# Softmax sums inverted in the attention stage, outputs scaled on GpSimd, and the layer norm moved into the group plan of a fused attention and recurrent-FFN kernel

## The chip, the cores and the metric

The kernel runs on one core of a Trainium2 chip. The metric is the device time of one execution in microseconds, the median of the runs shown. The engines are TensorE (PE, with its weight loads as PEld), VectorE (DVE), ScalarE (ACT), GpSimd (POOL) and SyncE (SP), which issues most of the DMAs. The kernel is written out by hand per engine: each engine has its own program, and semaphores order them.

## The reference, cut to what matters

Input x has 4 sequences of 1024 tokens with 1024 features. All of it is float32.

```python
xn = layernorm(x)
# attention: 32 query heads, 8 key/value heads, head size 32, rotary, causal
q, k, v = xn @ wq.T, xn @ wk.T, xn @ wv.T        # q, k rotated
attn = softmax(mask(q @ k.T / sqrt(32)))
s = (attn @ v) @ wo.T
# recurrent FFN on the last token only
thought = layer_norm(xn)[:, -1] @ agg_w + agg_b
for _ in range(4):
    t = gelu(layer_norm(thought) @ d1_w + d1_b)
    thought = thought + t @ d2_w + d2_b
f = layer_norm(xn + sigmoid(xn @ gate_w + gate_b) * (thought @ bc_w + bc_b))
out = x + s * silu(f)
```

## The kernel before, in words

There are three stages, one after the other, each a block with its own buffers.

`project_phase` normalises x, transposes it, and computes q, k and v as sums of three products of rounded parts. It writes the transposed x (`xt_scratch`), q, k and v to DRAM. The change does not touch it.

`attention_phase` runs over 32 groups, a group being one sequence and one key/value head with its 4 query heads (GROUPS, L26). Two groups make a turn of the loop over `c`, four turns (8 groups) make one step `s` of the recurrent FFN, and there are 4 steps. A group has 36 slots. In each slot PE computes one block of scores (`stp`, L985), ACT takes its exponential into `pr` (L796), and whatever `PLAN_TEXT` (L68) lists for the slot follows: `mx` is a product for the row maxima of the next group (PE, L973 to L978) with its maximum on DVE (`row_max`, L861), `pv` the product of probabilities and values into `yp` (L992), `ss` the column sums of the probabilities into the PSUM tile `trp` (L1001), `mt` the transposed maxima, `cy` the copy of `yp` to `ys` on ACT (L765), `fa`/`fb`/`fs`/`ft` the pieces of the FFN's matrix-vector products, and `ge` the gelu on ACT. The maxima have two PSUM buffers (`mxp`): PE may compute maximum k only when DVE has finished k-2 (L969). The scores have two buffers as well. `trp` is one buffer that all of `ss`, `mt`, `fa`, `fb`, `ft` and the layer norm's means share in a fixed order, counted by `tr_full` and `tr_free`; `use` (L564) gives each its number.

POOL adds up the probabilities over the key blocks (`acc`, `acc0`; L721, L739, L749), and `ss` turns the result into sums. ACT copies the sums from `trp` to `sm` (`copy_sums`, L771), and SP stores them to DRAM (`s_scratch`, L607). The outputs `ys` are stored without being divided (`store_y`, L611).

The layer norm of the recurrent state (`th`, 128 x 32 numbers) lies between two steps, outside the plan: after the last group of a step DVE runs `layernorm_sum`, `layernorm_centre` and `layernorm_scale` (L952 to L956), PE multiplies the two sums by a matrix of 1/1024 (`mean`, L1134), and POOL raises the variance to the power -1/2 (`ln_pool`, L712). The result `t_in` is what `fa` needs in slot 3 of the next group.

`output_phase` first loads and splits the two weight matrices in 16 pieces through 4 staging buffers, and then runs over 32 tiles of 128 tokens. For a tile, PE computes `gp` = xn @ gate_w and `op` = y @ wo.T (48 products each, L1385). POOL's queue loads `xa` (the two parts of the transposed x, 1 MB) when `gp` of the tile before is done, and `yr` (the attention output, 0.5 MB) after the second `power` (L1273 to L1279). `xa` has one buffer, `gp` and `op` have two. SP loads x itself (`xs`) and stores the output. The softmax sums are handled here: SP loads 32 rows of sums (`load_sums`), DVE inverts them (`invert`, L1306), SP stores the inverses to `r_scratch` and reads them back spread over 128 partitions (`spread`, L1216, 0.5 MB into `o_rinv`), and DVE multiplies `yr` by them (`normalise`, L1312). Then ACT rounds `yr` into `ya[0]`, and DVE takes the rest into `ya[1]` (L1373), which `op` of the next tile needs. All of DVE's work on a tile stands in one fixed order (L1349 to L1373).

Of the kernel before, what the change touches and what calls it, by code (L numbers as in the profile page):

```python
# [82 lines left out]
14: ss 1  # L83
15: mx 7
16: mx 8
18: mx 9
19: mx 10, ge
20: ss 0, mx 11
# [3 lines left out]
24: pv 1 2  # L92
# [4 lines left out]
31: mx 18, pv 1 4  # L97
33: mx 19
# [23 lines left out]
TRN = 7  # L122
A0 = 6


def build_kernel(nc, x, wqT, wkT, wvT, woT, in_g, in_b, agg_w, agg_b, pn_g, pn_b, d1_w, d1_b, d2_w, d2_b,
# [11 lines left out]
    with ExitStack() as outer:  # L138
        def osb(name, shape, dt):
# [11 lines left out]
        s_d = dram("s_scratch", (REP, 1 + GROUPS, T), F32)  # L151
        r_d = dram("r_scratch", (2, REP * KV, P), F32)
        attention_phase(nc, x, in_g, in_b, agg_w, agg_b, pn_g, pn_b, d1_w, d1_b, d2_w, d2_b, bc_b, pick,
                        q_d, k_d, v_d, y_d, s_d, ident, ident16, mask_q, mask_k, mhalf, bcast)
        output_phase(nc, x, woT, gate_w, gate_b, out_g, out_b, xt_d, y_d, s_d, r_d, ident, mhalf, bcast, out)
# [317 lines left out]
def attention_phase(nc, x, in_g, in_b, agg_w, agg_b, pn_g, pn_b, d1_w, d1_b, d2_w, d2_b, bc_b, pick,  # L473
                    q_d, k_d, v_d, y_d, s_d, ident, ident16, mask_q, mask_k, mhalf, bcast):
# [7 lines left out]
    with ExitStack() as ctx:  # L482
# [18 lines left out]
        sm = [sb(f"sm{i}", [P, HALF], F32) for i in range(2)]  # L501
# [37 lines left out]
        s_out = [sem(f"a_s_out{i}") for i in range(2)]  # L539
# [10 lines left out]
        ln_sum, ln_ve, ln_rs = sem("a_ln_sum"), sem("a_ln_ve"), sem("a_ln_rs")  # L550
# [13 lines left out]
        use = {"fa": 0, ("mt", 1): 1, "fb": 2, "ft": 3, ("ss", 1): 4, ("ss", 0): 5, ("mt", 0): 6}  # L564
# [6 lines left out]
        def _(sp):  # L571
# [35 lines left out]
            def store_sums(half, slot):  # L607
                sp.dma_start(s_d[:, bass.ds(slot, 1), half * HALF:(half + 1) * HALF].rearrange("h a t -> h (a t)"),
                             sm[half][0:P:HD, :]).then_inc(s_out[half], 16)

# [23 lines left out]
            load_w(0, d1_chunk(0))  # L634
            sp.wait_ge(tr_full, 4)
            load_w(1, d1_chunk(0))
# [3 lines left out]
            with sp.Fori(0, STEPS) as s:  # L640
                with sp.Fori(0, CH) as c:
                    for par in range(2):
                        it = s * CH + c
                        n = it * 2 + par
                        nxt = 1 - par
                        tb = trb(s, c, par)
                        sp.wait_ge(st_done, NST * n + 2)
                        load_k(nxt, (n + 1) % GROUPS)
                        load_q(1, nxt, it if par == 0 else (it + 1) % (GROUPS // 2))
                        sp.wait_ge(pv_done, products((1, 7), n))  # L650
                        load_v(nxt, (n + 1) % GROUPS)
                        sp.wait_ge(ys_done, 2 * n + 2)
                        store_y(1, n)
# [813 lines left out]
```

## Time and profile before

| | us |
|---|---|
| median of 3 runs (lowest, highest) | 2888.37 (2877.07, 2893.84) |
| the profiled execution, its own time | 2904.24 |
| the profiled execution's span | 2902.5 |
| PE busy | 2643.2 (91%) |
| DVE busy | 1714.5 (59%) |
| POOL busy | 1297.7 (45%) |
| ACT busy | 1055.4 (36%) |

The projection takes about the first 600 us of the span, the attention stage lasts to about 1990, and the output stage, with its weights first, to the end. The page gives the shares over the whole span; each stage has to be read by itself, with the view that lists the busy time of each engine by stretch. PEclk is the granted clock of TensorE as a share of the full one.

### The profile page before, as it was taken

The numbers are of one execution on the slowest core, as the hardware profiler recorded it, in microseconds if no ns is written. First come the engines' busy times: TensorE is split into PE (matmuls) and PEld (weight loads), VectorE is DVE, ScalarE is ACT, GpSimd is POOL, SyncE is SP. The second block draws the span as 40 slices with busy tenths as digits, with TensorE's granted clock in tenths as the row PEclk, the third lists the DMA queues.
The fourth block names the chain that finished last, engine by engine and source line by source line (L and its number), as shares of the span: only waits on it lengthen the run. The fifth ranks groups of instructions, "written<-read, shape, count | busy, mean of one in ns | idle before, by whom it ended". The sixth has DMA issues, their size and how long they took to land. (4 is left out here: it accounts for less than half of the span.)

```text
span 2902.5 us, 46017 instructions
## 1 busy us (share of the span) xinstructions
PE 2643.2 (91%) x14400; PEld 1712.5 (59%) x14400; DVE 1714.5 (59%) x3448; ACT 1055.4 (36%) x1715; POOL 1297.7 (45%) x562
## 2 busy tenths in 40 slices
PE   5999999969999999999999999995688788898887
PEld 4888888844444444444444444442577676676775
DVE  6455444356555655566556655653666667676666
ACT  2111111106666565665666556662211111111111
POOL 0211211127788678877888688872111111111111
PEclk9999999979999999999999999997799999899998
DMA  6444444365654565556455545564678677567766
GB/s 232 167 175 172 166 173 174 138 201 182 189 154 152 166 189 153 153 167 186 152 156 167 184 152 157 167 189 137 138 123 116 111 123 123 111 124 124 123 114 121
DMA packets 235894, 450.04 MB, mean 155 GB/s; under 512 B 17528, under 2 KB 101720, under 8 KB 235860
## 3 DMA queue, kind: packets, MB, share of 16 engines
q1 hardware_dynamic: 162468, 397.68, 43.3%
q0 software_dynamic: 73392, 51.91, 14.4%
q8 instruction: 21, 0.34, 0.0%
q14 instruction: 13, 0.11, 0.0%
HBM read 334.42 MB, written 114.58 MB: 155 GB/s over the span
## 5 line engine op out<-in xcount | busy, mean ns | idle before, releaser
L867 DVE CUSTOM_DVE_ANT_0 bcast<-mxp,mask_q 128x128 f32<-128x128 f32 (+7 forms) x1054 | 751.9, 754 | 506.4 <-PE mxp L976 283.5
L796 ACT ACTIVATE pr<-stp 128x512 f32<-128x512 f32 x1152 | 670.3, 596 | 529.1 <-PE stp L985 351.6
L985 PE MATMUL stp<-qs,ks 97*128 97x512 f32 x1152 | 522.5, 461 | 19.2 <-ACT pr L796 14.8
L1385 PE MATMUL gp<-g,xa 128*128 128x512 f32 x1536 | 395.3, 421 | 128.9 <-DMA xa<-xt_scratch 117.5
L426 PE MATMUL eo<-xt,w 128*128 128x512 f32 x1920 | 449.2, 393 | 3.6 <-DVE xt L369 3.6
L749 POOL TENSOR_TENSOR acc<-acc,pr 128x2048 f32<-128x2048 f32 x96 | 439.7, 4580 | 24.7 <-ACT pr L796 14.5
L985 PEld LDWEIGHTS stp<-qs,ks 97*128 97x128 f32 x1152 | 214.7, 189 | 384.1 <-ACT pr L796 275.8
L1385 PEld LDWEIGHTS gp<-g,xa 128*128 128x128 f32 x1536 | 313.5, 206 | 210.1 <-issue 108.0
L426 PEld LDWEIGHTS eo<-xt,w 128*128 128x128 f32 x1920 | 359.1, 189 | 77.5 <-issue 4.0
L1385 PE MATMUL op<-o,ya 128*128 128x512 f32 x1536 | 356.2, 391 | 21.6 <-DVE ya L1326 21.6
L1385 PEld LDWEIGHTS op<-o,ya 128*128 128x128 f32 x1536 | 290.3, 189 | 82.6 <-DVE ya L1326 22.0
L997 PE MATMUL yp<-pr,vs 128*32 128x512 f32 (+3 forms) x3088 | 323.1, 498 | 0.0
L1258 POOL DMA_DIRECT2D xa<-xt_scratch x66 | 57.6, 878 | 540.5 <-PE gp L1385 447.2
L975 PE MATMUL mxp<-ks,qs 96*128 96x512 f32 x526 | 244.8, 465 | 3.4 <-DVE mx L867 3.2
L721 POOL TENSOR_TENSOR acc<-acc,pr 128x1536 f32<-128x1536 f32 (+2 forms) x99 | 235.3, 2377 | 16.5 <-PE yp L1077 9.0
L749 POOL TENSOR_TENSOR acc<-pr 128x2048 f32<-128x2048 f32 x32 | 146.7, 4585 | 175.2 <-ACT pr L796 175.2
L291 POOL TENSOR_TENSOR r<-rt,r 128x1024 fp32r<-128x1024 f32 x40 | 95.9, 2398 | 282.1 <-ACT r L322 282.1
L395 DVE TENSOR_TENSOR rt<-eo,cs 128x512 f32<-128x512 f32 x160 | 99.0, 680 | 147.3 <-PE eo L426 147.3
L976 PE MATMUL mxp<-ks,qs 96*128 96x256 f32 (+2 forms) x526 | 172.1, 327 | 0.0
L322 ACT ACTIVATE r<-rt 128x1024 fp32r<-128x1024 f32 x40 | 42.4, 1061 | 356.7 <-DVE rt L399 356.7
L1296 ACT ACTIVATE c<-a 128x1024 f32<-128x1024 f32 x32 | 33.9, 1058 | 343.6 <-DVE a L1363 343.6
L978 PE MATMUL mxp<-ks,qs 96*128 96x256 f32 (+2 forms) x528 | 132.8, 354 | 18.3 <-DMA qs<-q_scratch 16.5
(139 smaller groups left out, 2788.0 us busy)
## 6 DMA issues: line engine op xcount, KB each, us to landing
wch<-in_d_w SPq DMA_DIRECT2D x132, 1024.0 KB, 8.0
qs<-q_scratch SPq DMA_DIRECT2D x201, 256.0 KB, 7.3
xa<-xt_scratch POOLq DMA_DIRECT2D x66, 512.0 KB, 9.0
xt_scratch<-xt SPq DMA_DIRECT2D x16, 2048.0 KB, 14.6
q_scratch<-r SPq DMA_DIRECT2D x64, 512.0 KB, 3.2
o_rinv<-r_scratch SPq DMA_DIRECT2D x33, 512.0 KB
yr<-y_scratch POOLq DMA_DIRECT2D x33, 512.0 KB, 6.5
xs<-in_x SPq DMA_DIRECT2D x33, 512.0 KB, 10.7
```

Of the source, the lines that this page charges most:

```text
L395: last = nc.vector.tensor_tensor(rt[:, o, :], bank[:, e, :], cs[:, s, tok], ALU.mult)
L426: last = nc.tensor.matmul(out, lhs[a](k), rhs[c](k), start=(k == 0 and (a, c) == (0, 0)), stop=(k == KT - 1 and (a, c) == (1, 0)))
L721: nc.gpsimd.tensor_tensor(acc[:, :, c0:HALF], acc[:, :, c0:HALF], pr[1][:, :, at:at + HALF - c0], ALU.add).then_inc(add_done, 1)
L749: nc.gpsimd.tensor_tensor(acc[:], other, pr[1][:, :, at:at + HALF], ALU.add).then_inc(add_done, 1)
L796: nc.scalar.activation(pr[half][:, :, at:at + P], stp[u % 2][:].rearrange("p (h t) -> p h t", h=REP), ACT.Exp, scale=SCALE).then_inc(act_d ...
L867: last = nc.vector.tensor_tensor_reduce(out=bcast[:, k % 2, hh * step:hh * step + w], in0=mxp[k % 2][:, hh * step:hh * step + w], in1=mask ...
L975: nc.tensor.matmul(bank[:, 0:512], lhs, ks[par][0:QR, 0:512], start=True, stop=True)
L976: last = nc.tensor.matmul(bank[:, 512:512 + w], lhs, ks[par][0:QR, 512:512 + w], start=True, stop=True)
L978: last = nc.tensor.matmul(bank[:, hh * step:hh * step + w], lhs, ks[par][0:QR, 0:w], start=True, stop=True)
L985: last = nc.tensor.matmul(bank, ks[par][:, j * P:(j + 1) * P], qs[par][:, :, i * P:(i + 1) * P], start=True, stop=i != j)
L997: last = nc.tensor.matmul(yp[h * HD:(h + 1) * HD, c0:HALF], vs[par][:, j, :], pr[half][:, h, at:at + HALF - c0], start=(j == 0), stop=(j = ...
L1385: last = nc.tensor.matmul(bank[:, cols], lhs[pa][:, k, :], ws[pw][:, k, cols], start=(k == 0 and (pa, pw) == (0, 0)), stop=(k == KT - 1 an ...
```

## The change

- Attention stage. `copy_sums` and `store_sums` are gone, with `sm`, `s_scratch` and `r_scratch`. DVE gets a plan entry `rc` right behind `ss` (slots 14 and 20): a 32x32-block transpose of `trp` (128x512, PSUM) to SBUF, a reciprocal of every 32nd column (16 per partition), and a second 32x32 transpose that reads those 16 numbers broadcast 32 times and writes `rinv` (128x512).
- POOL multiplies `ys` by `rinv` in place (`normalise`), half 1 after its first addition of half 1 and half 0 after the second. SP stores `ys` when that is done, so `store_y` moves behind the second weight burst in SP's order, and one follows `move_mt(0)`.
- The layer norm becomes plan entries of the last group of a step: `ls` in slot 15, `l0` and `lc` in 18, `l1` and `lv` in 24, `lt` in 32. `ln_pool` stands behind POOL's third addition of half 1. For this the loops run over CH-1 turns and the last turn is written out (`turns`).
- SP loads the next keys and queries one score block earlier. The weights of the FFN are still loaded by SP.
- Output stage. `load_sums`, `spread`, `invert` and `normalise` are gone. POOL's order becomes: wait for `y2_done`, load `yr`, wait for `g_done`, load `xa`, the two powers.

The core of the diff (the re-indentation of the loop bodies is left out):

```diff
-14: ss 1
-15: mx 7
+14: ss 1, rc 1
+15: mx 7, ls
-18: mx 9
+18: mx 9, l0, lc
-20: ss 0, mx 11
+20: ss 0, rc 0, mx 11
-24: pv 1 2
+24: pv 1 2, l1, lv
+32: lt
...
+        uses = [{"fa": 0, ("mt", 1): 1, "fb": 2, "ft": 3, ("ss", 1): 4, ("ss", 0): 5, ("mt", 0): 6},
+                {"fa": 0, ("mt", 1): 1, "fb": 2, "ft": 3, ("ss", 1): 4, "l0": 5, ("ss", 0): 6, "l1": 7, ("mt", 0): 8}]
...
@@ SP, one group
+                sp.wait_ge(st_done, NST * n + 1)
...
-                        sp.wait_ge(ys_done, 2 * n + 2)
-                        store_y(1, n)
...
-                        sp.wait_ge(ys_done, 2 * n + 3)
-                        store_y(0, n + 1)
-                        sp.wait_ge(tr_free, tb + use[("ss", 1)] + 2)
-                        store_sums(1, n)
-                        sp.wait_ge(tr_free, tb + use[("ss", 0)] + 2)
-                        store_sums(0, n + 1)
+                sp.wait_ge(yn_done, 2 * n + 3)
+                store_y(1, n)
                 sp.wait_ge(tr_free, tb + use[("mt", 0)] + 2)
                 move_mt(0, nxt)
+                sp.wait_ge(yn_done, 2 * n + 4)
+                store_y(0, n + 1)
@@ POOL
+            def normalise(half, n):
+                pool.wait_ge(ys_done, 2 * n + 3 - half)
+                pool.wait_ge(rc_done, 2 * n + 2 - half)
+                nc.gpsimd.tensor_tensor(ys[half][:], ys[half][:], rinv[half][:], ALU.mult).then_inc(yn_done, 1)
...
                     nc.gpsimd.tensor_tensor(acc[:], other, pr[1][:, :, at:at + HALF], ALU.add).then_inc(add_done, 1)
+                    if j == 1:
+                        normalise(1, n)
+                    if j == 2:
+                        normalise(0, n)
+                    if j == 3 and "l1" in use:
+                        ln_pool(s + 1, tb + use["l1"])
@@ DVE
+            def reciprocals(half, k, tu):
+                dve.wait_ge(tr_full, tu + 1)
+                nc.vector.transpose(sq_t[:].rearrange("p a u -> p (a u)"), trp[:]).then_inc(tr_free, 1)
+                dve.wait_ge(tr_free, tu + 2)
+                nc.vector.reciprocal(rr[half][:], sq_t[:, :, 0]).then_inc(rr_done, 1)
+                dve.wait_ge(yn_done, 2 * k + 2 - half)
+                dve.wait_ge(rr_done, 2 * k + 2 - half)
+                nc.vector.transpose(rinv[half][:], rr[half][:].unsqueeze(2).to_broadcast([P, SPREAD, SQUARE])
+                                    ).then_inc(rc_done, 1)
...
+                        elif e[0] == "rc":
+                            reciprocals(e[1], n, tb + use[("ss", e[1])])
...
+                        elif e[0] == "ls" and "l0" in use:
+                            link(nc.vector.tensor_tensor(th[:], th[:], bc(fvec[:, 3, :], B), ALU.add), base)
+                            layernorm_sum()
+                        elif e[0] == "lc" and "l0" in use:
+                            layernorm_centre(tb + use["l0"], base)
+                        elif e[0] == "lv" and "l1" in use:
+                            layernorm_var(tb + use["l1"])
+                        elif e[0] == "lt" and "l1" in use:
+                            layernorm_scale(s + 1, base)
@@ output stage, POOL
             with pool.Fori(0, TILES) as n:
+                pool.wait_ge(y2_done, n + 1)
+                load_ya((n + 1) % TILES)
                 pool.wait_ge(g_done, n + 1)
                 load_xa((n + 1) % TILES)
                 power(n, 0)
                 power(n, 1)
-                pool.wait_ge(y2_done, n + 1)
-                load_ya((n + 1) % TILES)
@@ output stage, SP and DVE
-                    spread(1 - par, n + 1)
-                    load_sums((n + 2) % TILES)
...
-                    invert(n + 1)
...
-                    normalise(n + 1)
```

## Rows read from the trace of the kernel before

**Rows 1.** Busy time by stretch (us, PE, PEld, DVE, ACT, POOL, clock, DMA share, GB/s).
```profile
760.00:1070.00 310.00, 301.66 (x1909) 141.31 (x1908) 186.43 (x509) 186.66 (x331) 246.60 (x78) 0.98 0.52 160
2052.00:2902.50 850.50, 729.34 (x3024) 591.74 (x3024) 567.67 (x672) 121.01 (x111) 124.44 (x158) 0.92 0.70 118
```

**Rows 2.** Timeline of PE, output stage: start, duration, engine, line, operation, idle before.
```profile
2065.61 11.04 PE L1385 MATMUL gp<-g,xa 128*128 128x512 f32 x48
...
2256.10 12.61 PE L1385 MATMUL gp<-g,xa 128*128 128x512 f32 x48 [6.86 <-DMA xa<-xt_scratch]
2279.90 11.17 PE L1385 MATMUL gp<-g,xa 128*128 128x512 f32 x48 [0.30 <-DMA xa<-xt_scratch]
...
2864.90 11.04 PE L1385 MATMUL gp<-g,xa 128*128 128x512 f32 x48
```

**Rows 3.** The chain of work that ended last, output stage (start, duration, what).
```profile
2003.96 12.91 DMA c<-in_gate_w
...
2240.23 15.74 DMA xa<-xt_scratch
...
2270.58 9.27 DMA xa<-xt_scratch
```

**Rows 4.** Timelines of SP, POOL and DVE, two tiles of the output stage and the end.
```profile
2239.17 0.56 SPq L1221 DMA_DIRECT2D o_rinv<-r_scratch  x1
2241.23 0.41 SPq L1242 DMA_DIRECT2D xs<-in_x  x1
...
2239.37 1.74 POOL L1258 DMA_DIRECT2D xa<-xt_scratch  x2 [12.22 <-PE gp L1385]
2248.27 1.11 POOL L1263 DMA_DIRECT2D yr<-y_scratch  x1 [0.21 <-issue]
...
2257.54 1.22 DVE L1315 TENSOR_TENSOR yr<-yr,o_rinv 128x1024 f32<-128x1024 f32 x1 [6.11 <-DMA yr<-y_scratch]
2291.11 1.23 DVE L1352 TENSOR_TENSOR a<-gp,vecs 128x1024 f32<-128x1024 f32 x1 [0.54 <-PE gp L1385]
2302.90 1.22 DVE L1363 TENSOR_TENSOR a<-a,vecs 128x1024 f32<-128x1024 f32 x1
2894.52 1.22 DVE L1315 TENSOR_TENSOR yr<-yr,o_rinv 128x1024 f32<-128x1024 f32 x1 [5.42 <-DMA yr<-y_scratch]
```

**Rows 5.** Groups by line and shape (count | busy us, mean ns | idle before).
```profile
L874 DVE TENSOR_TENSOR fsb<-trp,fsb 128x512 f32<-128x512 f32 x22 | 15.2, 691 | 10.4 <-PE trp L1029 10.4
L1310 DVE RECIPROCAL o_rcp<-ident 32x128 f32<-32x128 f32 x32 | 29.9, 933 | 0.0
L739 POOL TENSOR_TENSOR acc<-acc,pr 128x512 f32<-128x512 f32 x22 | 28.4, 1289 | 3.5 <-ACT pr L796 3.5
```

**Rows 6.** Timelines of DVE, PE and POOL, slots 15 to 18 of one group.
```profile
1041.12 0.82 DVE L867 CUSTOM_DVE_ANT_0 bcast<-mxp,mask_q 128x640 f32<-128x640 f32 x1 [0.23 <-PE mxp L976]
...
1042.24 0.50 PE L985 MATMUL stp<-qs,ks 97*128 97x512 f32 x1 [0.45 <-ACT pr L796]
1042.58 0.40 PE L975 MATMUL mxp<-ks,qs 96*128 96x512 f32 x1
...
1042.76 4.59 POOL L749 TENSOR_TENSOR acc<-pr 128x2048 f32<-128x2048 f32 x1 [5.48 <-ACT pr L796]
```

**Rows 7.** Timeline of ACT: the copy of slot 13 in three groups, all of parity 1.
```profile
949.34 0.59 ACT L769 ACTIVATE ys<-yp 128x512 f32<-128x512 f32 x1
...
1039.10 0.59 ACT L769 ACTIVATE ys<-yp 128x512 f32<-128x512 f32 x1
...
1119.78 0.59 ACT L769 ACTIVATE ys<-yp 128x512 f32<-128x512 f32 x1
```

**Rows 8.** Timelines of POOL and DVE in the layer norm between two steps.
```profile
974.92 7.28 POOL L721 TENSOR_TENSOR acc<-acc,pr 128x1536 f32<-128x1536 f32 x3
...
974.98 3.44 DVE L856 TENSOR_TENSOR cen<-cen,f_rs 128x32 f32<-128x32 f32 x1 [1.13 <-POOL f_rs L714]
978.46 2.39 DVE L858 TENSOR_TENSOR cen<-cen,fvec 128x32 f32<-128x32 f32 x1
```

More of the change, by code:

```diff
@@ L122 @@
 TRN = 7
+SQUARE = 32
+SPREAD = HALF // SQUARE
 A0 = 6
@@ L751, in _ @@
+            ln_pool(0, 6)
+            pool.wait_ge(init_p, 3)
+            turns(pool, turn)
             late_additions(GROUPS)
+            normalise(1, GROUPS)
         @block.scalar
@@ new lines, in turn @@
+            def turn(s, c, par, use):
+                it = s * CH + c
+                n = it * 2 + par
+                tb = trb(s, c, par)
+                for u, (half, j, i) in enumerate(ST):
+                    act.wait_ge(st_done, NST * n + u + 2)
+                    if u == 0:
+                        act.wait_ge(tr_full, tb)
+                    if u == HALF_ST:
+                        act.wait_ge(pv_done, NPV * n + 1)
+                        act.wait_ge(add_done, NADD * n + 1)
+                    if u == LAST_UNIT[(1, 4)] + 1:
+                        act.wait_ge(tr_full, tb + use[("ss", 1)] + 1)
+                    at, c0 = prob_piece(half, j)
+                    at += i * P - half * HALF - c0
+                    nc.scalar.activation(pr[half][:, :, at:at + P], stp[u % 2][:].rearrange("p (h t) -> p h t", h=REP),
+                                         ACT.Exp, scale=SCALE).then_inc(act_done, 1)
+                    for e in ACT_PLAN[u]:
+                        if e[0] == "fc":
+                            copy_burst(tb + use["fa"])
+                        elif e[0] == "cy":
+                            copy_y(e[1], n, products((1, 7) if e[1] else (0, 3), n))
+                        elif e[0] == "mt":
+                            if e[1] == 0:
+                                act.wait_ge(m_in[par], (it + 1) * 16)
+                            elif par == 1:
+                                act.wait_ge(m_in[2], (it + 1) * 16)
+                            else:
+                                act.wait_ge(st_done, n * NST + 1)
+                            max_rows(e[1], tb + use[e])
+                        elif e[0] == "ge" and par == 0:
+                            act.wait_ge(hp_done, it + 1)
+                            nc.scalar.activation(h_in[:, :, 0:B], hpre[:], ACT.Gelu).then_inc(h_done, 1)
@@ L958, in _ @@
+                if par == 1:
+                    assert links["n"] == LINKS_TURN + ("l0" in use) * LINKS_STEP, links["n"]
+            turns(dve, turn)
             nc.vector.tensor_copy(h_in[:, :, 0:B], th[:]).then_inc(t_done, 1)
@@ L1136, in _ @@
+            turns(pe, turn)
             pe.wait_ge(act_done, GROUPS * NST + A0)
@@ L1323, in _ @@
             dve.wait_ge(vec_in, 48)
-            normalise(0)
             dve.wait_ge(y1_done, 1)
```

401 lines of the change are left out of this document (158 added, 243 removed).

## The prediction

> **What bounds the kernel now.** I read the busy time by stretch first, then the PE timeline of each stage, then the chain of waits, then what the other engines and the DMA queues do around each wait of PE.
>
> In the attention stage PE is busy 301.66 of 310 us at a granted clock of 0.98; POOL has 246.60 and DVE 186.43 [rows 1]. So PE's program is the length of this stage, and an added wait of PE is added to the end. A group takes 80.68 / 2 = 40.3 us, and where a step ends, two groups take 89.76: the layer norm between two steps costs 9.1 us [rows 7].
>
> In the output stage PE is busy 729 of 850 us [rows 1]. From `gp` of tile 1 to `gp` of tile 31 there are 799.3 us, 26.64 per tile, while `gp` and `op` need about 10.9 each, 21.8 together, when nothing is late (the 11.04 of a row overlaps the next one by about 0.15) [rows 2]. The rest are waits for `xa`: they alternate, 6.86 us in one tile and 0.30 in the next, and after the long wait `gp` itself takes 12.6 in place of 11.0 [rows 2]. The chain shows the cause: the load takes 15.74 us in one tile and 9.27 in the next [rows 3]. In the slow one it shares the DMA engines with `o_rinv` (issued 2239.17) and `xs` (2241.23), both within 2 us of `xa` (2239.37) [rows 4]. `o_rinv` is what the change removes.
>
> **Output stage, the tiles.** A tile moves 3 MB now (`xa` 1, and 0.5 each for `yr`, `o_rinv`, `xs` and the store), 2.5 MB after. At 118 GB/s for a share of 0.70 [rows 1] full use is about 169 GB/s, so 2.5 MB keep the DMA engines busy for 15.5 us, less than 21.8: the tile can be PE's if the order is right. Does the new order collide? DVE takes 13.0 us from a finished `gp` to the end of L1363 (2291.11 to 2304.1) [rows 4]; then come a sigmoid on ACT (about 1) and four operations of 1.2 each, the last of which sets `y2_done`: 19 us after `gp`. In between `normalise` is gone, with the wait of 6.11 us that it had in slow tiles [rows 4]. So POOL issues `yr` at 19, 1.1 us of descriptors (L1263) [rows 4]; SP stores the output at 18 and loads `xs` when that has landed, at about 21; `xa` starts at the next `gp`'s end, 22 at the soonest. POOL is not held up: `y2_done` always comes before `g_done`.
>
> Bounds of the period T: below, 21.8. Above, 1.05 million bytes (`yr`, `xs`) are 6.2 us of DMA time; they have T - 20.5 us of lead before `xa`, what is left of them delays it, and `xa` needs 1.3 for issue and 9.3 to land [rows 3] while `op` covers 10.9. With w the wait and T = 21.8 + w, w = 1.3 + 9.3 + 6.2 - (T - 20.5) - 10.9, so w = 2.3 and T = 24.1. A longer wait heals itself, because `yr` and `xs` then lie further ahead. The tile that waited 0.30 us had `xs` and `o_rinv` just ahead of `xa` in the same way, so I stay nearer to the lower end: w = 0.8, T = 22.6. That is (26.64 - 22.6) x 30 = 121 us less; the ends are 145 and 76.
>
> **Output stage, both ends.** The third weight piece now waits behind the round trip of the first sums, issued at 2003.5 and landing 12.91 us later on the chain [rows 3]. Without it all four buffers fill at once, about 10 us sooner, but the same bytes must arrive: between 0 and 11, I take 6, and 1.2 for the first `normalise`. At the end `normalise` waits 5.42 us for a `yr` that no tile needs, then takes 1.22 itself; the sigmoid that stands beside it takes 1.1, so 5.5 us go [rows 4]. Together 13.
>
> **Attention stage, the sums.** ACT loses two copies of 0.6 us a group. That relieves PE once: the wait of 0.45 us for ACT in slot 18 stands behind the copy [rows 6]. DVE gains two `rc`. The trace has no transpose. Nearest below and of equal size is a 128x512 operation of DVE that reads PSUM, 0.69 us; above is the reciprocal, 0.93 us for 128 numbers [rows 5], at whose pace 512 would take about 3.3. A transpose computes nothing, so I take 0.69 each. 16 reciprocals are about 0.25, so an `rc` is 1.66 us with its hand-overs.
> The Trainium skill (Vector Engine (DVE) Microarchitecture Reference, "3.8 The reshape front-end and per-opcode configuration") has the transpose pipelined at one element per cycle and lane, which no row here shows; the sum by it is the same.
> What is queued behind `rc` matters more than its length. In slots 13 to 18 DVE goes from maximum to maximum: maximum 7 starts at 1041.12, only 0.23 us after maximum 6 [rows 6]. With `rc 1` between them it starts at 1042.6 and ends at 1043.45. PE's product 9 needs that buffer and now starts at 1042.58 [rows 6]; it moves to 1043.55, and product 10 behind maximum 8 by 1.1 us in all. `rc 0` in slot 20 finds PE busy with three long products and delays nothing by the same count (0.7 us to spare). So a group is 1.1 us longer, 0.75 in the groups of parity 0, where the gelu's table loads already hold PE for 0.37: 0.92 x 32 = 29 us more. Bounds: nothing, if the relief of ACT and slack I don't see absorb it, and 45 us at 0.9 us per transpose.
> POOL gains two multiplications of 1.29 us [rows 5]. In each group it waits 5.48 us before the first addition of half 1 [rows 6]; 2.58 us fit into that and cost nothing. With more than 5.5 us added, the exponentials and `ss` would wait for POOL, each us over it once a group. The later `store_y` costs nothing either: the copy that rewrites a half of `ys` comes most of a group (40.3 us) after the scaling.
>
> **Attention stage, the layer norm.** The wish is that 9.1 us per step go. Against it stands this: while POOL is in an addition, a DVE operation with both inputs in SBUF does not end before it. L856 on 128x32 numbers began at 974.98 and took 3.44 us, to 978.42, where POOL's first of three additions (7.28 us together) ended; L858 took 2.39 behind the second [rows 8].
> The Trainium skill says the same ("SBUF — State Buffer", "Who interferes with whom"): such an operation and a GpSimd one that reads SBUF exclude each other for a whole instruction. It is the rule that speaks against this change.
> Between two steps POOL was partly idle. In the plan it is not: `ls` comes up at 1043.4, in an addition that lasts from 1042.76 to 1047.35 [rows 6]. DVE stands for 3.6 us, PE waits at `l0` for the sum, and everything moves by some 4.8 us with the two means. `lt` comes up in slot 32 as POOL starts its fourth addition (4.6 us) and needs two or three such turns: 8 us, with maximum 19 behind it, and PE's product 21 behind that: 5 us. That is 9.8 us, and PE ran slower for a while after its waits, as `gp` shows (12.6 for 11.0) [rows 2]: 3 more. So a step end costs 13 in place of 9.1, +4 x 3 = +12. In the last step `h_in` is ready a few us sooner and `ls` costs its 4.8: +2. Bounds for the four: -33 if nothing waits, +35 if all the waits are in full.
>
> **Sum.** -121 - 13 + 29 + 12 + 2 = -91 us. The profiled execution took 2904.24, so 2813; the median of the runs shown lies 15.9 us below that execution, so 2888.37 - 91 = 2797.
>
> **Rivals.**
> A, the DMA engines collide in every tile (T = 24.6): -61 - 13 + 43 = -31, 2857. For it: 15.74 us of `xa` beside two other loads [rows 3, 4], and `yr` now goes ahead of `xa` in the same queue. Against it: the lead grows with the wait. Chance 0.16.
> B, the new work fits in the gaps: `rc` costs PE nothing and the layer norm's operations fall between POOL's. Attention -33, 2888 - 134 - 33 = 2721. For it: DVE is busy 60% of the stage [rows 1]. Against it: rows 6 and 8. Chance 0.16.
> C, slower than before: a transpose goes at the reciprocal's pace. With `rc` of R us PE loses R - 0.55 behind the first and R - 2.4 behind the second; at R = 6.8 that is 10.6 us a group, 340 in all, 2888 - 134 + 14 + 340 = 3108. It decides from 3.75 us a group, R = 3.35, 1.5 us per transpose. Chance 0.06.
> D, the change does its work but nothing is won: `xa` alone is what is slow, and the waits stay. Output -13, 2918, slower. Against it 9.27 beside 15.74 [rows 3]. Chance 0.02.
> My forecast has 0.6.
>
> **Range.** The forecast's own case spans 2760 to 2835, from T of 21.8 to 24.1 and the bounds in attention. With A and most of B it is 2725 to 2865. About 0.5% (14 us) is what a measurement of this kernel can tell from no change. Faster by more: the forecast, B and A but for its upper tail, 0.87; within: 0.05; slower: C, D and a part of A's tail, 0.08.
>
> **What would show it.** `gp` at 22 to 23 us per tile with waits for `xa` under 2 us and no alternation; `xa` landing in 9 to 12 us. A transpose of 0.6 to 0.75 us in the groups of DVE. The slot-13 copies 82.5 us apart over two groups (80.68 now), and about 95 across a step end; the `th` addition lasting until POOL's addition ends, and PE idle 3 to 4 us ahead of the first mean. I am wrong if transposes take over 1 us, if the copies stay at 80.7, or if `xa` still takes 15 us in every second tile.

## The result, and the profile after

The changed kernel takes 2796.09 us (median of 4 runs, 2793.21 to 2799.96); the kernel before, in the same comparison, 2885.57 (4 runs, 2877.07 to 2893.84). The ratio is 0.9699, 95% interval 0.967 to 0.9728: faster by 89.5 us. The forecast was 2797, so the number is right. Its two halves are not: the output stage won more than forecast and the attention stage lost more. That they cancel is luck.

| us | before | after | after minus before | forecast |
|---|---|---|---|---|
| span of the profiled execution | 2902.5 | 2791.2 | -111.3 | -91 |
| until SP issues the first load of the output stage | 1992.2 | 2053.6 | +61.4 | +43 |
| from there to the end | 910.3 | 737.6 | -172.7 | -134 |
| median of the runs | 2885.57 | 2796.09 | -89.5 | -91 |

The spans differ by 22 us more than the medians do. The profiled execution of before (2904.24) lay 18.7 us above its median and that of after (2793.21) 2.9 us below, so each part of -172.7 is read with that in mind. The first load is one of the old sums before and the first piece of the gate's weights after.

Busy time by stretch in the changed kernel: the stretch of [rows 1] in attention, and the output stage's tiles from 2 on. Columns as in rows 1.

```profile
760.00:1070.00 310.00, 292.89 (x1816) 136.96 (x1808) 206.39 (x532) 171.86 (x300) 249.72 (x87) 0.96 0.50 155
...
2127.92:2769.84 641.92, 641.92 (x2833) 531.53 (x2832) 464.39 (x557) 110.32 (x104) 110.36 (x146) 1.00 0.61 119
```

The last line is what to look at: over 642 us of the output stage TensorE is busy in every microsecond, at a granted clock of 1.00. Before it was 729 of 850 at 0.92 [rows 1]; that stretch takes in both ends of the stage, but from `gp` of tile 1 to `gp` of tile 31 alone it was 693.8 of 799.3, also at 0.92. The first line shows the price: in attention TensorE's idle time in 310 us went from 8.3 to 17.1.

The PE timeline of the output stage, beside [rows 2]:

```profile
2069.82 12.71 PE L1371 MATMUL gp<-g,xa 128*128 128x512 f32 x48 [17.60 <-DMA xa<-xt_scratch]
2093.45 12.87 PE L1371 MATMUL op<-o,ya 128*128 128x512 f32 x48 [10.92 <-DVE ya L1314]
2106.16 11.04 PE L1371 MATMUL gp<-g,xa 128*128 128x512 f32 x48
...
2758.96 11.04 PE L1371 MATMUL gp<-g,xa 128*128 128x512 f32 x48
2769.84 11.04 PE L1371 MATMUL op<-o,ya 128*128 128x512 f32 x48
```

From `gp` of tile 1 (2106.16) to `gp` of tile 31 (2758.96) there are 652.8 us, 21.76 per tile, with no wait in any of them: the stage stands at the floor of its matrix products. The loads of a tile, from the DMA issues of this stretch (KB each, median us to landing):

```profile
xa<-xt_scratch POOLq DMA_DIRECT2D x60, 512.0 KB, 6.2
...
yr<-y_scratch POOLq DMA_DIRECT2D x30, 512.0 KB, 5.9
xs<-in_x SPq DMA_DIRECT2D x30, 512.0 KB, 5.5
```

In attention, the copies of slot 13 on ACT (the three that answer to [rows 7]). Two of these copies that are two groups apart make an interval; a regular one has no step end in it:

```profile
957.57 0.59 ACT L781 ACTIVATE ys<-yp 128x512 f32<-128x512 f32 x1
...
1055.52 0.59 ACT L781 ACTIVATE ys<-yp 128x512 f32<-128x512 f32 x1
...
1137.87 0.59 ACT L781 ACTIVATE ys<-yp 128x512 f32<-128x512 f32 x1
```

Two groups take 82.35 us (80.68 before), two with a step end between them 97.95 (89.76 before): the end of a step costs 15.6 us here and 15.1 on the mean of the three, each counted by the intervals between copies against a regular pair. It was 9.1 here and 8.7 on the mean before.

The groups by shape that are new on DVE (count, busy us and mean ns, idle time before), for attention:

```profile
L869 DVE STREAM_TRANSPOSE sq_t<-trp 128x512 f32<-128x512 f32 x65 | 46.4, 714 | 14.7 <-PE trp L1029 12.0
L874 DVE STREAM_TRANSPOSE rinv<-rr 128x512 f32<-128x512 f32 x65 | 46.2, 711 | 7.3
L871 DVE RECIPROCAL rr<-sq_t 128x16 f32<-128x16 f32 x65 | 16.5, 253 | 2.2
```

And where they stand, in one group: the timeline of DVE from slot 14, and PE's wait that follows.

```profile
832.76 0.71 DVE L869 STREAM_TRANSPOSE sq_t<-trp 128x512 f32<-128x512 f32 x1
833.51 0.25 DVE L871 RECIPROCAL rr<-sq_t 128x16 f32<-128x16 f32 x1
833.87 0.71 DVE L874 STREAM_TRANSPOSE rinv<-rr 128x512 f32<-128x512 f32 x1
834.51 0.79 DVE L883 CUSTOM_DVE_ANT_0 bcast<-mxp,mask_q 128x640 f32<-128x640 f32 x1
...
835.37 0.50 PE L998 MATMUL mxp<-ks,qs 96*128 96x512 f32 x1 [0.98 <-DVE mx L883]
```

`rc 1` stands between maxima 6 and 7 and PE waits 0.98 us for a buffer of `mxp`. There is something here that I had not counted. In 7 of the 32 groups the stretch from a slot-13 copy to the next slot-3 copy is 28.1 to 28.4 us instead of 26.7 to 26.8. One of them, by windows, and PE's wait ahead of it:

```profile
876.60 0.51 PE L998 MATMUL mxp<-ks,qs 96*128 96x512 f32 x1 [1.07 <-DVE mx L883]
```

```profile
876.00:878.00 2.00, 1.40 (x6) 0.97 (x6) 1.88 (x5) 0.67 (x2) 2.00 (x1) 1.00 1.03 412
878.00:880.00 2.00, 2.00 (x18) 0.68 (x18) 1.30 (x5) 0.69 (x2) 2.00 (x1) 0.62 1.01 402
880.00:882.00 2.00, 2.00 (x11) 0.81 (x14) 1.85 (x4) 0.60 (x1) 1.64 (x3) 0.52 0.07 12
```

TensorE is busy all through 878 to 882, but at a granted clock of 0.62 and 0.52: the wait of 1.07 us ended at 876.60, the clock was still 1.00 up to 878, and then TensorE ran some 3 us at the lower of its two levels (1.2 GHz of 2.4). That makes a wait of 1 us cost 2.5 where it happens. Why it happens in these seven groups and not in the others, which have the same wait, no run shows.

The end of a step, timelines of POOL, DVE and PE, beside [rows 8]:

```profile
961.02 4.50 POOL L751 TENSOR_TENSOR acc<-pr 128x2048 f32<-128x2048 f32 x1 [5.26 <-ACT pr L800]
...
961.77 3.80 DVE L968 TENSOR_TENSOR th<-th,fvec 128x32 f32<-128x32 f32 x1
...
983.83 3.91 DVE L861 TENSOR_TENSOR cen<-cen,f_rs 128x32 f32<-128x32 f32 x1
987.78 3.48 DVE L862 TENSOR_TENSOR cen<-cen,fvec 128x32 f32<-128x32 f32 x1
991.30 2.38 DVE L863 TENSOR_TENSOR t_in<-cen,fvec 128x32 f32<-128x32 f32 x1
...
965.87 0.59 PE L1068 MATMUL trp<-s,onesd 128*128 128x4 f32 x2 [3.35 <-DVE s L846]
989.44 0.50 PE L1008 MATMUL stp<-qs,ks 97*128 97x512 f32 x1 [2.89 <-issue]
994.88 0.79 PE L998 MATMUL mxp<-ks,qs 96*128 96x512 f32 x1 [2.96 <-DVE mx L883]
```

`ls` (L968) stands behind POOL's addition until 965.5, `lt` (L861 to L863) for 9.8 us, and PE waits for DVE as forecast, though for less at `lt`: 3.35 us (3 to 4 forecast) and 2.96 us (5 forecast). The wait of 2.89 us for "issue" ahead of the first score tile of a step is the second thing not counted: the profile names no engine and no DMA for it. Before, the three such waits were 1.4 us together, now 8.3.

Busy time by stretch from one slot-13 copy to the next across the first step end, in the kernel before and in the changed one:

```profile
949.34:998.55 49.21, 44.24 (x263) 20.34 (x262) 32.08 (x78) 23.95 (x44) 33.59 (x11) 0.90 0.46 141
957.57:1014.40 56.83, 46.48 (x263) 21.27 (x262) 41.51 (x84) 23.11 (x42) 35.79 (x13) 0.85 0.38 122
```

PE's idle time in it went from 5.0 to 10.4 us. The granted clock is below 1.00 in both: a step end was paid in part by the lower clock already before (0.90 of 49.2 us is 5 us of full clock missing; regular groups of before have 1.00), and the new waits lengthened that stretch (0.85 of 56.8 us, 8.5 missing).

### The profile page after: what moved, and what is told of

Read it like the earlier page. It is cut to its first block and busy times, and to the rows that moved or that the text cites. A ratio compares the mean times of both kernels' runs of the same rounds, so it can differ in the third digit from the quotient of the medians.

```text
span 2791.2 us, 45646 instructions
## 1 busy us (share of the span) xinstructions
PE 2627.8 (94%) x14400; PEld 1695.3 (61%) x14400; DVE 1771.3 (63%) x3577; ACT 1028.3 (37%) x1650; POOL 1369.2 (49%) x627
## 5 line engine op out<-in xcount | busy, mean ns | idle before, releaser
L883 DVE CUSTOM_DVE_ANT_0 bcast<-mxp,mask_q 128x128 f32<-128x128 f32 (+7 forms) x1054 | 751.3, 752 | 430.0 <-PE mxp L1001 212.0
L1371 PE MATMUL gp<-g,xa 128*128 128x512 f32 x1536 | 355.0, 390 | 17.6 <-DMA xa<-xt_scratch 17.6
L1371 PEld LDWEIGHTS gp<-g,xa 128*128 128x128 f32 x1536 | 289.4, 188 | 78.6 <-DMA xa<-xt_scratch 18.4
L998 PE MATMUL mxp<-ks,qs 96*128 96x512 f32 x526 | 255.9, 487 | 42.6 <-DVE mx L883 42.5
L1265 POOL DMA_DIRECT2D yr<-y_scratch x33 | 30.5, 924 | 364.2 <-issue 334.8
L998 PEld LDWEIGHTS mxp<-ks,qs 96*128 96x128 f32 x526 | 103.1, 196 | 129.0 <-DVE mx L883 122.5
L999 PE MATMUL mxp<-ks,qs 96*128 96x256 f32 (+2 forms) x526 | 174.1, 331 | 0.0
```

The costliest lines, as they stand in the source:

```text
L883: last = nc.vector.tensor_tensor_reduce(out=bcast[:, k % 2, hh * step:hh * step + w], in0=mxp[k % 2][:, hh * step:hh * step + w], in1=mask ...
L998: nc.tensor.matmul(bank[:, 0:512], lhs, ks[par][0:QR, 0:512], start=True, stop=True)
L999: last = nc.tensor.matmul(bank[:, 512:512 + w], lhs, ks[par][0:QR, 512:512 + w], start=True, stop=True)
L1371: last = nc.tensor.matmul(bank[:, cols], lhs[pa][:, k, :], ws[pw][:, k, cols], start=(k == 0 and (pa, pw) == (0, 0)), stop=(k == KT - 1 an ...
```

## The experiments: the attention stage

All times are medians, each beside runs of the kernel before on the same chip. These differ a little by chip (2883.97 us beside the first four, 2880.04 beside a_both, a_split_loop and o_late, 2884.86 beside the other kernels of the output stage), so a few us between two kernels that ran on different chips are read by the ratios. The ratios are to before; the changed kernel's own is 0.9699. The expectations call it "after".

**a_split** moves the half of `rc` that nobody in slots 14 to 20 waits for, the reciprocal and the second transpose. With it GpSimd's two scalings come one addition later, and `sq_t` gets a second buffer.

```
-        sq_t = sb("sq_t", [P, SPREAD, SQUARE], F32)
+        sq_t = [sb(f"sq_t{i}", [P, SPREAD, SQUARE], F32) for i in range(2)]
-23: mx 13
+23: mx 13, ri 1
-26: mx 15
+26: mx 15, ri 0
...
-                nc.vector.transpose(sq_t[:].rearrange("p a u -> p (a u)"), trp[:]).then_inc(tr_free, 1)
+                nc.vector.transpose(sq_t[half][:].rearrange("p a u -> p (a u)"), trp[:]).then_inc(tr_free, 1)
+
+            def spread_inverse(half, k, tu):
                 dve.wait_ge(tr_free, tu + 2)
-                nc.vector.reciprocal(rr[half][:], sq_t[:, :, 0]).then_inc(rr_done, 1)
+                nc.vector.reciprocal(rr[half][:], sq_t[half][:, :, 0]).then_inc(rr_done, 1)
...
-                    if j == 1:
-                        normalise(1, n)
                     if j == 2:
+                        normalise(1, n)
+                    if j == 3:
                         normalise(0, n)
```

> The changed kernel, with the reciprocal and the second transpose of each rc moved to slots 23 and 26, where VectorE idles 1.1 to 1.3 us in the trace of after, and GpSimd's two scalings one addition later. Theory (what each group pays is the 1.66 us of rc between the maxima, which delays units 9 and 10): TensorE's wait of 0.98 us ahead of unit 9 falls under 0.3, a regular group from 41.2 us to about 40.3, the seven groups with a dip of the granted clock (28.1 to 28.4 us instead of 26.8 in their second part) lose it: 32 x 0.9 + 10 = 39 us less than 2796, about 2757. Rival 1 (GpSimd's scaling is what costs, through the port it shares or its own 1.27 us): groups stay at 41.1 to 41.2, about 2796. Rival 2 (the moved pair delays units 14 and 16 instead, 0.96 each with 1.1 to 1.3 us of idle time there): about 2785 to 2800.

Measured: 2736.89 us, ratio 0.9493 (0.9466 to 0.9521), 59 us less than the changed kernel and 20 more than the theory gave. The DVE timeline of a group, and the maximum product's group on PE (the changed kernel's line reads 42.6 <-DVE mx L883 42.5):

```profile
827.54 0.71 DVE L869 STREAM_TRANSPOSE sq_t<-trp 128x512 f32<-128x512 f32 x1
...
837.01 0.25 DVE L873 RECIPROCAL rr<-sq_t 128x16 f32<-128x16 f32 x1
837.37 0.71 DVE L876 STREAM_TRANSPOSE rinv<-rr 128x512 f32<-128x512 f32 x1
838.35 1.09 DVE L885 CUSTOM_DVE_ANT_0 bcast<-mxp,mask_q 128x896 f32<-128x896 f32 x1 [0.27 <-PE mxp L1004]
```

```profile
L1003 PE MATMUL mxp<-ks,qs 96*128 96x512 f32 x526 | 255.2, 485 | 11.0 <-DVE mx L885 9.2
```

The moved pair ends 0.27 us before DVE's next product is there, so it fits in the gap. The intervals between copies are 14.43 + 25.60 and 14.43 + 26.05 in turn, 80.5 us over two groups; before it was 80.68. So the net price of the inversion in a regular group is gone, with both transposes, the reciprocal, POOL's two scalings and the stores all still there. It is a net price: PE's wait for ACT in each group (14.8 us in 32 waits before) is gone with the copies of the sums, in the changed kernel too, so up to 0.4 us a group may still be paid. The intervals refute rival 1 and rival 2. The edit moves POOL's scalings as well, but the wait that fell, from 42.5 to 9.2 us, is PE's for the maxima on DVE; so it was the position of 0.96 us of DVE's work that cost. No interval of 28 us is left among the regular ones. The 20 us beyond the theory: the step ends went from 15.1 to 10.6 us on the mean of the three (-14), and the last group's stretch from 31.27 to 26.08 (-5).

**a_lnpool** takes the layer norm's two-input operations out of DVE's way.

```
-11: mx 4, ft
+11: mx 4, ft, ls
-15: mx 7, ls
+15: mx 7
...
+            def scale_pool(k):
+                g, b = (fvec[:, r, :].unsqueeze(2).to_broadcast([P, KT, B]) for r in (1, 2))
+                pool.wait_ge(ln_rs, k + 1)
+                nc.gpsimd.tensor_tensor(cen[:], cen[:], rs[:].unsqueeze(1).to_broadcast([P, KT, B]), ALU.mult).then_inc(lp, 1)
...
                         ln_pool(s + 1, tb + use["l1"])
+                        scale_pool(s + 1)
...
-                        elif e[0] == "lt" and "l1" in use:
-                            layernorm_scale(s + 1, base)
```

> The changed kernel, with ls moved from slot 15 to slot 11 (GpSimd idles there) and the three small operations of lt done by GpSimd itself behind the power. Theory (the layer norm is dear because VectorE's operations with two SBUF inputs stand behind GpSimd's additions, 3.8 us at ls and 9.8 us at lt, and TensorE then waits 3.35 and 2.96 us and runs at the lower clock after them): both waits go, a step end costs some 5 us instead of 15.6 (the 2.9 us of issue ahead of the first score tile stay): 3 x 10 = 30 us less than 2796, about 2766. Rival (the 15 us come from the second copy of the turn in the program and the longer plan, not from the waits for VectorE): no more than 5 us less, 2791 or above.

Measured: 2771.15 us (2762.61 to 2781.54), ratio 0.9601 (0.9567 to 0.9634), 25 us less. The waits for the mean and ahead of unit 21 are gone, and the operations cost what their size says:

```profile
958.84 0.19 DVE L979 TENSOR_TENSOR th<-th,fvec 128x32 f32<-128x32 f32 x1
...
982.09 0.24 POOL L721 TENSOR_TENSOR cen<-cen,f_rs 128x32 f32<-128x32 f32 x1
...
988.74 0.50 PE L1017 MATMUL stp<-qs,ks 97*128 97x512 f32 x1 [2.68 <-issue]
```

3.80 us became 0.19, and the three operations of 9.77 us became three of 0.24 on POOL. That confirms where the layer norm's waits came from; the rival (at most 5 us) falls. But a step end costs 10.1 us, not 5. The gap of 2.68 for issue stays, and so does the wait behind `rc 1`. The lower clock stays as well: across the first step end PE is idle for only 4.0 of 51.05 us, fewer than before, yet at a granted clock of 0.87. The profiled execution is the slowest of the four (2781.54). In it 15 regular stretches were longer than 28 us, where that of the changed kernel had 7. The wait of 1 us that comes ahead of them is there in both, so how often the clock falls behind it is not settled by the wait alone.

**a_between and a_between_loop** put the layer norm back between the steps, once with the last turn of a step still written out a second time, once as a single loop.

The edit of both (PE's part; DVE and POOL have an `end` of the same kind):

```
                 for par in range(2):
                     turn(s, CH - 1, par, uses[par])
+                if end:
+                    end(s)
...
+            def end(s):
+                for k, v in enumerate((s1, s2)):
+                    mean(TR0 + s * TR_STEP + NT * TRN + k, v, (s + 1) * 2 + k + 1)
```

What a_between_loop changes beyond it:

```
-                with engine.Fori(0, CH - 1) as c:
+                with engine.Fori(0, CH) as c:
                     for par in range(2):
                         turn(s, c, par, uses[0])
-                for par in range(2):
-                    turn(s, CH - 1, par, uses[par])
```

> The changed kernel, with the whole layer norm back between two steps as before, but the last turn of each step still written out a second time. Theory: a step end costs what it cost before (8.6 to 9.1 us in place of 14.1 to 15.7) plus the gap of 2.9 us for issue, if that belongs to the second copy of the turn: 3 x (15.1 - 8.9 - 2.9) = 10 us less than 2796, about 2786. If the gap belongs to something else it is gone here as well, 2778. Rival (layer norm in the plan is cheaper than between steps, and the excess has another source): 2796 or more.

> As a_between, and the turns as one loop again, so that only the sums' inversion, the scaling and the output stage differ from the kernel before. If the second copy of the turn costs the 2.9 us of issue at each step end, it is 9 us faster than a_between, about 2777, and the gap ahead of the first score tile of a step is gone from the trace; if the copy costs nothing, both agree within 3 us.

Measured: a_between 2791.45 us, ratio 0.9674 (0.9644 to 0.9704); a_between_loop 2784.73, ratio 0.9664 (0.9636 to 0.9693). The order is the expected one, the sizes are smaller (5 and 11 us for 10 and 19), and the intervals of the two overlap; the verdict rests on the traces. The traced execution of a_between_loop is its fastest (2772.28, 12 us under the median), with 7 stretches of 28 us to a_between's 12, so only the wait is compared, not the span. PE's waits for issue, in total, how many and the longest, in a_between:

```profile
PE stp L1020 <- issue: 16.3, 3, 6.0
```

and in a_between_loop:

```profile
PE stp L1018 <- issue: 1.3, 3, 0.5
```

In the changed kernel they are 8.3 us, in the kernel before 1.4. So the gap belongs to the second copy of the turn in the program, shown by the one edit that takes the copy away; a_split (8.4) and a_split_loop below (0.7) show it again. What fills the gap is not shown by a row. The queue of instruction loads is a hint, no more. In the changed kernel (packets, MB, share):

```profile
q8 instruction: 58, 0.95, 0.1%
```

With the single loop q8 has 21 packets and 0.34 MB, as before. Step ends on the mean: a_between 14.0 us, a_between_loop 10.6, where 8.9 had been expected. So with the second copy in both, the layer norm in the plan (15.1) was no better than between the steps (14.0).

**a_both** is a_split with a_lnpool.

> a_split and a_lnpool together. a_split took 59 us off the changed kernel (2737) and a_lnpool 25 (2771). If they take away different things: 2737 - 25 = 2712. But a_split shortened the step ends too (35.3 + 15.2 to 16.4 us in place of 39.5 to 40.8 + 16; 10.4 us over a regular pair in place of 15.2) and the last group by 5 us, which a_lnpool also won; what is left for lt on GpSimd is then TensorE's last wait of 0.5 us and the 4.5 + 3.5 us of VectorE behind GpSimd's additions ahead of units 20 and 21: 3 x 3 = 9 us, about 2728. I take the second. It would be the fastest so far.

Measured: 2727.72 us (2727.05 to 2729.68), ratio 0.9473 (0.9457 to 0.9489), the value expected (2728) from what a_split had already taken of a_lnpool's gain. It beats both kernels, by 5.3% and 2.3%. Of the 9 us by which its median is under a_split's some 4 are the chip's (before: 2883.97 and 2880.04); by the traces the step ends took 3. A step end costs 9.6 us; some 3 of them are the gap for issue (3.05 at the first).

**a_split_loop** asks whether the layer norm in the plan pays once DVE is in time. Its edit is a_split's and a_between_loop's.

> a_split with the layer norm back between the steps and the turns as one loop, that is the attention stage of before with the inversion and GpSimd's scaling in it. Its regular groups cost what they did before (40.3 us), so this asks whether the layer norm in the plan pays once VectorE is no longer late. Theory: a step end costs 9.0 us as before, against 10.4 in a_split, 3 x 1.4 = 4 us less than 2737, about 2733: what the plan wins in waits for the layer norm it gives back with the second copy of the turn. Rival: without the backlog the plan's layer norm is the better one, and this is 2745 or more.

Measured: 2738.83 us, ratio 0.9509 (0.9493 to 0.9525), against 0.9493 for a_split: the same within the intervals, 6 us over the theory's 2733 and 6 under the rival's 2745. A step end costs 11.4 us with the layer norm between the steps and 10.6 in the plan. It falls between theory and rival and settles neither. So moving the layer norm into the plan by itself won nothing that can be measured; only with the operations off DVE (a_both, on the same chip) is it ahead, by 11 us.

## The experiments: the output stage

**o_order, o_dma, o_dve** each put one part of the output stage back into the changed kernel.

The edit of o_order:

```
-                pool.wait_ge(y2_done, n + 1)
-                load_ya((n + 1) % TILES)
                 pool.wait_ge(g_done, n + 1)
                 load_xa((n + 1) % TILES)
                 power(n, 0)
                 power(n, 1)
+                pool.wait_ge(y2_done, n + 1)
+                load_ya((n + 1) % TILES)
```

Of o_dma (one more such read goes out ahead of the weights):

```
+            rows = r_d.rearrange("(h g) t -> h (g t)", h=REP).unsqueeze(1).to_broadcast([REP, HD, KV * P])
...
+                    sp.wait_ge(ri_in, m * 32 + 16 * par + 16)
+                    sp.dma_start(spare[:], rows).then_inc(ri_in, 16)
                     sp.wait_ge(out_done[1 - par], m * 16 + 1 if par == 0 else m * 16 + 17)
```

Of o_dve (`rinv` holds ones):

```
+                nc.vector.tensor_tensor(yr[:], yr[:], rinv[:], ALU.mult).then_inc(yn_done, 1)
...
+                    nc.vector.reciprocal(rcp[:], bcast[0:REP * KV, 0, 0:P]).then_inc(rc_done, 1)
...
-                    act.wait_ge(ya_in, 16 * (n + 2))
+                    act.wait_ge(yn_done, n + 2)
```

> The changed kernel with GpSimd's old order in the output stage: xa's loads and the two powers ahead of yr's load. Theory (the gain of the output stage is the read of o_rinv and VectorE's chain for it, the order of the loads only moves yr within its slack): a tile stays at 21.8 to 22.2 us, 2796 to 2808. Rival (xa comes in time only because yr is loaded ahead of it): xa's landing goes to 8 us or more and a tile to 23 or above, 32 x 1.2 = 38 us more, 2834.

> The changed kernel with one broadcast read of 0.5 MB per output tile put back in SyncE's queue (into a buffer that nobody reads), ahead of xs. Theory (the read shares the DMA engines with xa, which TensorE waited for in 5 to 9 us per pair of tiles before): xa lands in about 9 us instead of 6.2, TensorE waits for it and a tile takes 24 to 26.5 us: 32 x 2.2 to 4.7 = 70 to 150 us more, about 2900. Rival (TensorE waited because VectorE's chain held the tile up, and the transfer was hidden): 21.8 to 22.3, 2796 to 2812.

> The changed kernel with VectorE's work for the sums put back in the output stage, with no transfer: a reciprocal (0.7 us) at the head of the tile and the multiply of yr (0.9 to 1.3 us) between the load of yr and ScalarE's copy. Theory (VectorE has 2.5 us idle per tile of 21.8, and the chain of yr has room): a tile takes 21.8 to 22.4, 2796 to 2816. Rival (the chain through VectorE was the bound of before): 24 to 26.6, 2870 to 2950.

| kernel | median us | ratio to before (95%) | us per tile, 1 to 31 |
|---|---|---|---|
| changed kernel | 2796.09 | 0.9699 (0.967 to 0.9728) | 21.76 |
| o_order | 2797.65 | 0.969 (0.9653 to 0.9727) | 21.76 |
| o_dve | 2796.79 | 0.9698 (0.9659 to 0.9737) | 21.76 |
| o_dma | 2898.92 | 1.0043 (1.0024 to 1.0061) | 24.72 |
| o_all | 2897.54 | 1.0043 (1.0013 to 1.0073) | 24.55 |
| o_late | 3000.85 | 1.041 (1.0382 to 1.0438) | 28.26 |

The order of the loads and DVE's chain through `yr` cost nothing: their kernels show `gp` and `op` 10.88 us apart throughout. The read alone gives back 103 us and brings the alternation of before back. PE timeline of o_dma:

```profile
2124.15 11.04 PE L1381 MATMUL gp<-g,xa 128*128 128x512 f32 x48
...
2148.54 12.79 PE L1381 MATMUL gp<-g,xa 128*128 128x512 f32 x48 [2.47 <-DMA xa<-xt_scratch]
...
2865.72 11.04 PE L1381 MATMUL gp<-g,xa 128*128 128x512 f32 x48
```

and its DMA issues in the tiles:

```profile
xa<-xt_scratch POOLq DMA_DIRECT2D x54, 512.0 KB, 9.5
yr<-y_scratch POOLq DMA_DIRECT2D x27, 512.0 KB, 11.0
xs<-in_x SPq DMA_DIRECT2D x27, 512.0 KB, 11.6
```

`xa` lands in 9.5 us instead of 6.2. That nobody reads what the transfer brings makes the reading strict: it is the transfer itself, and no engine's wait on its data. Whether it meets `xa` in the DMA engines or in the memory behind them is not told apart. Over these tiles the busy share of the DMA engines is only 0.72, so it is bunching, not volume. A slow tile, from the timelines of SP and POOL:

```profile
2228.62 0.54 SPq L1253 DMA_DIRECT2D o_spare<-r_scratch  x1
2231.21 0.34 SPq L1255 DMA_DIRECT2D xs<-in_x  x1
...
2232.35 1.74 POOL L1270 DMA_DIRECT2D xa<-xt_scratch  x2 [1.33 <-PE gp L1381]
```

The read goes out 3.7 us ahead of `xa` here, with `yr` (2230.10) and `xs` between them. In the next tile, where nobody waits, it is 10.4 us ahead. Every second tile waits 2.5 to 5.3 us, and its `gp` then takes 12.6 to 14.0 us for 11.04. (2865.72 - 2124.15) / 30 = 24.72 per tile, 2.96 more than 21.76: 89 us. The start of the stage gives some 12 more: it takes 52.3 us from SP's first issue to the first `op` (2059.31 to 2111.57), where the changed kernel takes 39.9; 2 of them pass before the first gate weight is issued, in the small store that this kernel makes once.

**o_all** puts back all three. It multiplies by another array than the inverted sums, so its output is another one; only its time is of use.

> All three put back in the output stage: the old order, the 0.5 MB read and VectorE's two operations (the multiply takes a row of bcast in place of the inverted sums, so the output is scaled by another factor). Theory: with everything back a tile takes what it took before, 26.6 us, so that 32 x 4.9 = 156 us come on top of 2796: 2950. What is missing to that is due to the small loads of the sums, the store and the wait between them.

Measured 2897.54 us: no more than o_dma, and 52 short of 2950. Three things of before are still missing here, the small store, the small load and the wait between them, and with them the moment at which the read goes out. **o_late** changes the moment. It does not change it alone: SP works in order, so `xs`, which follows the read, moves beside `xa` too, and the store of the output now waits until the read has landed.

Its edit against o_dma:

```
-                    sp.wait_ge(ri_in, m * 32 + 16 * par + 16)
+                    sp.wait_ge(g_done, n + 1)
                     sp.dma_start(spare[:], rows).then_inc(ri_in, 16)
...
                     sp.wait_ge(a_done, n + 1)
+                    sp.wait_ge(ri_in, 16 * (n + 2))
```

> o_dma with the 0.5 MB read held until the gate's product of the tile is done, so that it goes out beside xa as o_rinv's did before (0.2 us apart in rows 4), not with out of the tile before. o_dma brought back 103 us of what the output stage had won (tiles of 24.5 us), and o_all no more (2897.5); 26.6 us per tile of before would be 2950. Theory (the rest is due to when the read goes out): tiles of 26 to 27 us, 2935 to 2955. Rival (the read costs the same whenever it goes out, and the rest came from the small store and loads of the sums and the waits between them): about 2899, 24.5 us per tile.

Measured: 3000.85 us, 102 above o_dma and 46 above the upper end of what I expected. Timelines of SP, POOL and PE for one tile:

```profile
2275.28 0.55 SPq L1253 DMA_DIRECT2D o_spare<-r_scratch  x1
2276.14 0.35 SPq L1255 DMA_DIRECT2D xs<-in_x  x1
...
2276.03 1.74 POOL L1271 DMA_DIRECT2D xa<-xt_scratch  x2 [7.00 <-PE gp L1382]
...
2291.59 13.42 PE L1382 MATMUL gp<-g,xa 128*128 128x512 f32 x48 [5.45 <-DMA xa<-xt_scratch]
```

With the read and `xs` within 1 us of `xa`, `xa` takes 12.0 us on the median and every tile from 2 on waits 3.5 to 5.7 us, 28.26 us per tile. The extra read cost 3.0 us per tile sent 3.7 and 10.4 us ahead of `xa`, and 6.5 sent beside it together with `xs`; how the difference divides between the read and `xs` was not measured. The tiles of before, 26.64, lie between: there `o_rinv` went out 0.2 us ahead of `xa` in the tile of [rows 4], with `xs` 1.9 us behind it, and 3.9 us ahead in the next. So the read by itself is shown for 3.0 of the 4.9 us per tile, and the moment at which it and `xs` go out is large enough for the other 1.9. That the small transfers add nothing was not measured.

## Why the prediction came out, step by step

- **What bounds the two stages.** Right. Attention: a wait of PE is added to the end, every microsecond of it. Output: the waits for `xa`, made by `o_rinv` beside it; o_dma shows it for the larger part (3.0 of 4.9 us per tile). Of the 146 us that the tiles of before took over 21.76 each, 106 were the waits and 37 the slower `gp` after them, so a quarter of this price was slower products and not waiting (granted clock 0.92 over the stretch, 1.00 now).
- **Output tiles, -121 us (145 to 76).** Right in mechanism, too small. T is 21.76, a hair under the lower bound of 21.8, not 22.6: (26.64 - 21.76) x 30 = 146 us, up to 22 less if the profiled execution of before had its excess here. The step that failed is the choice of w = 0.8. I added the landing of 9.3 us from a tile of before, in which `o_rinv` and `xs` were still in the way; with them gone or done `xa` lands in 6.2, which `op` covers. The new order of `yr` and `xa` that I worked this wait out of turned out to be free either way (o_order).
- **Output ends, -13.** The tail is right: 21.4 us from the start of the last `op` to the end instead of 26.7, 5.4 less (5.5 forecast). The start is not: 39.9 us from SP's first issue to the first `op` instead of 59.7, 19.8 less where I had 7.2. I took the weights as bound by their bytes and let only part of the round trip go. In o_dma one such read and its store ahead of the weights cost 12, so the 0.5 MB of `spread` itself, which I left out of that sum, is the likely term. Before, the read went out behind the first two pieces, so what it cost there is not shown.
- **The transposes.** 0.714 and 0.711 us for my 0.69, the reciprocal 0.253 for 0.25. The Trainium skill (Vector Engine (DVE) Microarchitecture Reference, "3.8 The reshape front-end and per-opcode configuration") has a transpose sustain one element per cycle and lane. The trace fits that: a transpose of 128x512 took 0.71 us, an addition of the same size 0.69 [rows 5].
- **`rc` in the groups, +29.** Right: the pairs of groups took 82.35 us for 80.68, 0.84 per group, 27 in all, by the wait of PE ahead of product 9 that I named. a_split confirms place and cause. Missing was that TensorE's clock falls after such a wait in some groups: 7 stretches of 1.5 us, +10.
- **POOL's scaling and the later stores, nothing.** Right within the 0.4 us a group that a_split leaves open.
- **Layer norm in the plan, +12 for three and +2 for the last.** The mechanism is right as far as it goes, and the sign too: `th` stood 3.80 us (3.6), PE waited 3.35 for the mean (3 to 4), `lt` took 9.77 (8), and a_lnpool took these away. The size is short: step ends 15.1 for my 13, against 8.7 before, +19; the last group's stretch grew 6.1 us, 5 of them beyond a regular group's share. Inside the 13 the terms were off both ways. I had 9.8 of waits and 3 for the lower clock. Of the 15.6 us of the first step end the waits that I named are 6.3 (3.35 and 2.96), the gap for issue is 2.9, and some 6 are left, for the lower clock and PE's own work on the means. The term I left out is the second copy of the turn (a_between_loop), and the one I made too small is the clock.
- **The sum.** Attention +61 (27 + 10 + 19 + 5) for +43. The output stage won 172.7 by the spans for 134; as the spans exceed the medians by 22 us in their difference, 150 to 173 is what the runs allow. 18 us too much optimism in one stage met 16 to 39 too much pessimism in the other. The time was forecast within 1 us by luck; its terms were off by up to 25.
- **Rival B** (the work fits in the gaps) did not happen, but its reasoning was sound: DVE has the room in a regular group, as a_split shows, only not in slots 14 to 20. **Rivals A and D** fall with T = 21.76, **rival C** with 0.71 us per transpose.

## What to carry to other kernels

Split a step added to a tight engine at the point where others wait for it, and put the rest where that engine idles: here 0.96 us, moved by six and by nine slots in a group, was worth 59 us, about two thirds of the change's own gain. Before a broadcast read is called hidden, look at what goes out within a few microseconds of it: a busy share of 0.72 did not keep 0.5 MB from costing 3.0 us per tile. And when a forecast of several terms hits, check the terms: these were wrong in both directions.

## What the runs showed that I had not expected

- A wait of PE of about 1 us was followed in 7 of 32 groups by some 3 us at a granted clock of 0.5 to 0.6, so that it cost 2.5 us. At the step ends, too, part of the price was the lower clock: 0.90 over the group before, 0.85 now.
- Writing the last turn of a loop out a second time made PE stand 2.9 us for issue at each return to the first copy (8.3 us for three), and with the layer norm between the copies up to 6.0 (16.3 us for three); with one copy 1.3 us for three.
- The same 128x32 operation with two inputs in SBUF took DVE 3.80 us during an addition of POOL, 0.19 with POOL idle; one of the same size took POOL itself 0.24.
- A read of 0.5 MB that cost 3.0 us per tile cost 6.5 when it and the load that follows it in SP's queue went out beside `xa` instead of ahead of it.
